# Attention scores from two fp32r pieces in 64-row tiles instead of three bf16 pieces

## The reference

```python
qkv = x @ W_qkv + b_qkv                      # 16 heads, q, k, v of 16 columns each
q, k = rope(q), rope(k)                      # adjacent pairs turned by position
att = softmax(where(causal, q @ k.T / 4, -1e9))
x = layernorm(x + (att @ v) @ W_proj + b_proj)
# 8 experts, the likeliest one for each token, at most 640 tokens each
h = relu(dispatch @ w1[e] + b1[e])           # 256 -> 1024
x = layernorm(x + prob * (h @ w2[e] + b2[e]))
```

## Time and profile before

| | |
|---|---|
| span of the profiled execution | 1587.9 us |
| median of three runs | 1589.46 us |
| PE busy | 1348.4 us (85%) |
| DVE busy | 1197.6 us (75%) |
| ACT busy | 801.6 us (50%) |
| POOL busy | 341.8 us (22%) |
| mean granted TensorE clock | 0.893 |

### The profile page before, as it was taken

One profiled execution on the slowest core, in us unless ns is written; L12 is line 12 of the kernel. 1 busy time (PEld: TensorE's weight loads), 2 busy tenths in 40 slices (PEclk: granted clock), 3 DMA queues, 4 the chain that ended last, 5 costly groups with the idle time before them and its releaser, 6 DMA issues. The chain is left out here.

```text
span 1587.9 us, 26808 instructions
## 1 busy us (share of the span) xinstructions
PE 1348.4 (85%) x7840; PEld 665.9 (42%) x7840; DVE 1197.6 (75%) x2805; ACT 801.6 (50%) x1130; POOL 341.8 (22%) x310
## 2 busy tenths in 40 slices
PE   6766299999998998998999999999577839999987
PEld 3434111233232232332333333321156639999987
DVE  6997499797896887996887978940067638888896
ACT  3443100465665565665665666678534434444442
POOL 3555500001011001001010010110233423344442
PEclk9887555798999999999999999999888759999998
DMA  4586591001202102112002012000245541422220
GB/s 165 175 196 226 147 138 24 2 28 47 63 28 68 43 30 80 37 45 83 27 29 81 28 43 66 8 22 8 72 152 182 172 134 46 128 88 89 85 90 22
DMA packets 117979, 126.95 MB, mean 80 GB/s; under 512 B 14428, under 2 KB 100447, under 8 KB 117856
## 3 DMA queue, kind: packets, MB, share of 16 engines
q1 hardware_dynamic: 114272, 116.97, 25.8%
q0 software_dynamic: 3584, 8.47, 1.5%
HBM read 82.98 MB, written 48.38 MB: 83 GB/s over the span
## 5 line engine op out<-in xcount | busy, mean ns | idle before, releaser
L622 ACT ACTIVATE probs<-scores 128x1024 f32<-128x1024 f32 (+3 forms) x640 | 540.6, 896 | 413.7 <-PE scores L524 413.0
L669 DVE TENSOR_REDUCE part_max<-ring 128x1 f32<-128x512 f32 x768 | 484.4, 685 | 34.2 <-PE ring L552 32.2
L552 PE MATMUL ring<-k_stack,q_stack 96*128 96x512 bf16 (+3 forms) x1280 | 433.8, 384 | 61.9 <-DMA k_stack<-pieces_d 28.4
L524 PE MATMUL scores<-q_stack,k_stack 99*128 99x512 bf16 (+3 forms) x1280 | 344.2, 358 | 13.2 <-ACT probs L622 6.5
L542 PE MATMUL out_p<-probs,v_s 128*32 128x512 f32 (+3 forms) x2560 | 305.7, 550 | 9.3 <-POOL probs L714 5.9
L664 DVE CUSTOM_DVE_ANT_0 scratch<-ring,mask_s 128x384 f32<-128x384 f32 (+3 forms) x512 | 229.3, 488 | 99.3 <-issue 87.1
L552 PEld LDWEIGHTS ring<-k_stack,q_stack 96*128 96x128 bf16 x1280 | 120.7, 99 | 414.4 <-DVE part_max L669 170.1
L714 POOL TENSOR_SCALAR_AFFINE_SELECT probs<-probs 128x512 f32<-128x512 f32 x128 | 81.2, 634 | 863.6 <-ACT probs L622 863.6
L524 PEld LDWEIGHTS scores<-q_stack,k_stack 99*128 99x128 bf16 x1280 | 113.7, 100 | 170.7 <-ACT probs L622 68.1
L1353 PE MATMUL psH<-x_hi,w_hi 128*128 128x384 f32 (+1 forms) x256 | 85.6, 334 | 25.3 <-DVE x_lo L1454 21.9
L195 PE MATMUL psP<-xT,wqk_s 128*128 128x512 f32 x128 | 72.2, 728 | 35.2 <-ACT xT L234 31.4
(11 more groups left out here) (117 smaller groups left out, 1562.9 us busy)
## 6 DMA issues: line engine op xcount, KB each, us to landing
w_whole<-w SPq DMA_DIRECT2D x16, 1024.0 KB, 7.9
q_stack<-pieces_d SPq DMA_DIRECT2D x192, 64.0 KB, 2.7
k_stack<-pieces_d SPq DMA_DIRECT2D x192, 64.0 KB, 2.8
v_d<-vt SPq DMA_DIRECT2D x8, 1024.0 KB, 4.4
v_s<-v_d SPq DMA_DIRECT2D x8, 1024.0 KB, 5.9
o_d<-o_s SPq DMA_DIRECT2D x32, 256.0 KB, 2.1
p_o<-o_d SPq DMA_DIRECT2D x8, 1024.0 KB, 5.8
slots_d<-no_row SPq DMA_DIRECT2D x1, 5200.0 KB, 29.8
```

Source lines behind the costliest of these rows:

```text
L524: last = nc.tensor.matmul(scores[p][:, hh, off:CHUNK], k_stack[i][0:KROWS, j, kb * P:(kb + 1) * P], q_stack[i][0:KROWS, j, c * CHUNK + off ...
L552: nc.tensor.matmul(ring[m % 3][:, 0:w], q_stack[i][0:SROWS, j, qt * P:(qt + 1) * P], k_stack[i][0:SROWS, j, t * CHUNK:t * CHUNK + w], star ...
L622: nc.scalar.activation(probs[n % 2][:, 2 * p:2 * p + 2, off:CHUNK], scores[p][:, :, off:CHUNK], ACT.Exp, scale=SCALE).then_inc(exp_done[p], 1)
L669: nc.vector.tensor_reduce(out, ring[m % 3][:, 0:w], axis=AX.X, op=ALU.max).then_inc(ring_read, 1)
```

## The change

Query and key are cut in two fp32r pieces, and three products (hi-hi, hi-low, low-hi) take the place of six. 48 rows of products and 2 of maxima are 50, so a head fits in 64 rows; heads `2p` and `2p+1` stand in the lower and upper half of the partitions, and the two score matmuls of a pair, or two neighbouring maxima jobs, use different halves of TensorE's rows.

In the projection `mid` and both functions that make it (`rest` on VectorE, `cut_mid` on ScalarE) are gone; `low` is made straight from `raw` and `hi`. Since GpSimd now reads `raw` late, ScalarE waits before it overwrites it. SP stores two pieces of 4 bytes in place of three of 2.

In attention the fold is one reduction; its f32 result is transposed once, and VectorE cuts the transposed rows in two pieces. The rows of ones are written by eight DMAs from a small tile instead of GpSimd's memset. The order of jobs and steps, the plan, the ring and the widths are the same.

```diff
-TERMS = [(0, 0), (0, 1), (1, 0), (1, 1), (0, 2), (2, 0)]
+TERMS = [(0, 0), (0, 1), (1, 0)]
-NPIECE = 3
+NPIECE = 2
+HALF = P // 2
+NPAIR = HPU // 2
 # project_qkv
+            sp.sem_inc(low_ready, 2 * QKG)
-                for n, (ready, piece) in enumerate(((hi_ready, hi), (mid_ready, mid), (low_ready, low))):
+                for n, (ready, piece, start) in enumerate(((hi_ready, hi, 0), (low_ready, low, 2 * QKG))):
             def evacuate(b, c, g):
+                if g == 0:
+                    act.wait_ge(low_ready, QKG * (n + 1))
-                        if g:
-                            cut_mid(b, c, g - 1)
-                    cut_mid(b, c, QKG - 1)
-                if g:
-                    rest(b, c, g - 1)
-                pool.wait_ge(mid_ready, QKG * n + g + 1)
-                nc.gpsimd.tensor_tensor(low[i][:, g, :], rots[i][:, g, :], mid[i][:, g, :],
+                pool.wait_ge(hi_ready, QKG * n + g + 1)
+                nc.gpsimd.tensor_tensor(low[i][:, g, :], raw[i][:, g, :], hi[i][:, g, :],
                                         ALU.subtract).then_inc(low_ready, 1)
 # attention
-        q_stack = [sb(f"q_stack{i}", [P, HPU, T], BF16) for i in range(2)]
+        q_stack = [sb(f"q_stack{i}", [P, NPAIR, T], F32R) for i in range(2)]
-                    rows = slice(r * HS, (r + 1) * HS)
+                    for par in range(2):
+                        rows = slice(par * HALF + r * HS, par * HALF + (r + 1) * HS)
                     for hh in range(2):
-                        j = 2 * p + hh
+                        rows = slice(hh * HALF, hh * HALF + KROWS)
                         last = nc.tensor.matmul(scores[p][:, hh, off:CHUNK],
-                                                k_stack[i][0:KROWS, j, kb * P:(kb + 1) * P],
-                                                q_stack[i][0:KROWS, j, c * CHUNK + off:(c + 1) * CHUNK],
+                                                k_stack[i][rows, p, kb * P:(kb + 1) * P],
+                                                q_stack[i][rows, p, c * CHUNK + off:(c + 1) * CHUNK],
-                nc.tensor.matmul(ring[m % 3][:, 0:w], q_stack[i][0:SROWS, j, qt * P:(qt + 1) * P],
-                                 k_stack[i][0:SROWS, j, t * CHUNK:t * CHUNK + w],
+                rows = slice(j % 2 * HALF, j % 2 * HALF + SROWS)
+                nc.tensor.matmul(ring[m % 3][:, 0:w], q_stack[i][rows, j // 2, qt * P:(qt + 1) * P],
+                                 k_stack[i][rows, j // 2, t * CHUNK:t * CHUNK + w],
             def turn_maxima(u):
-                pe.wait_ge(pieces_ready, u + 1)
-                for s, pieces in enumerate(TURNED):
...
+                pe.wait_ge(fold, u + 1)
+                pe.wait_ge(ring_read, NRING * u + NMAX - 2)
+                nc.tensor.transpose(ring[NMAX % 3][:, 0:P], row_max[:], id_s[:]).then_inc(ring_full, 2)
 # fold_maxima, behind the reduction: four operations and two copies become
+                dve.wait_ge(ring_full, NRING * u + NMAX + 1)
+                turned = ring[NMAX % 3][0:HPU * NQT, 0:P]
+                nc.vector.tensor_scalar(max_rows[0][:], turned, -1.0, None, ALU.mult).then_inc(max_hi_ready, 1)
+                dve.wait_ge(max_hi_ready, u + 1)
+                nc.vector.scalar_tensor_tensor(max_rows[1][:], turned, -1.0, max_rows[0][:],
+                                               ALU.mult, ALU.subtract).then_inc(ring_read, 2)
```

More of the change, by code:

```diff
@@ L87, in project_qkv @@
         xcos = [sb(f"xcos{i}", [P, QKG, CHUNK]) for i in range(2)]
-        hi = [sb(f"hi{i}", [P, QKG, CHUNK], BF16) for i in range(2)]
-        mid = [sb(f"mid{i}", [P, QKG, CHUNK], BF16) for i in range(2)]
-        low = [sb(f"low{i}", [P, QKG, CHUNK], BF16) for i in range(2)]
+        hi = [sb(f"hi{i}", [P, QKG, CHUNK], F32R) for i in range(2)]
+        low = [sb(f"low{i}", [P, QKG, CHUNK], F32R) for i in range(2)]
         vt = [sb(f"vt{i}", [P, TPC, H, VW]) for i in range(2)]
@@ L299, in rope @@
                                         ALU.add).then_inc(roped, 1)
[L301 to L307, removed]
             with dve.Fori(0, B) as b:
@@ L407, in sem @@
             return ctx.enter_context(nc.semaphore(name))
-        q_stack = [sb(f"q_stack{i}", [P, HPU, T], BF16) for i in range(2)]
-        k_stack = [sb(f"k_stack{i}", [P, HPU, T], BF16) for i in range(2)]
+        q_stack = [sb(f"q_stack{i}", [P, NPAIR, T], F32R) for i in range(2)]
+        k_stack = [sb(f"k_stack{i}", [P, NPAIR, T], F32R) for i in range(2)]
         v_s = [sb(f"v_s{i}", [P, NQT, HPU * VW]) for i in range(2)]
@@ L456, in load_chunk @@
                 for r, (qp, kp) in enumerate(TERMS):
-                    rows = slice(r * HS, (r + 1) * HS)
-                    for stack, side, piece in ((q_stack, 0, qp), (k_stack, 1, kp)):
-                        sp.dma_start(stack[i][rows, :, cols],
-                                     pieces_d[b, piece, side, g, :, :, cols]).then_inc(stack_loaded[i][c], 16)
+                    for par in range(2):
+                        rows = slice(par * HALF + r * HS, par * HALF + (r + 1) * HS)
+                        for stack, side, piece in ((q_stack, 0, qp), (k_stack, 1, kp)):
+                            sp.dma_start(stack[i][rows, :, cols].bitcast(F32),
+                                         pieces_d[b, piece, side, g, par, :, :, cols]).then_inc(stack_loaded[i][c], 16)
             def load_v(b, g, i):
@@ L467, in load_max, with load_ones @@
                 for pc in range(NPIECE):
-                    at = (pc % 2) * HPU * NQT
-                    sp.dma_start(q_stack[i][SROWS + pc:SROWS + pc + 1],
-                                 max_rows[at:at + HPU * NQT, pc // 2, :]).then_inc(max_loaded[i], 16)
+                    for par in range(2):
+                        row = par * HALF + SROWS + pc
+                        sp.dma_start(q_stack[i][row:row + 1].bitcast(F32),
+                                     max_rows[pc][par * NPAIR * NQT:(par + 1) * NPAIR * NQT, :].bitcast(F32)
+                                     ).then_inc(max_loaded[i], 16)
+            def load_ones(i):
+                for pc in range(NPIECE):
+                    for par in range(2):
+                        row = par * HALF + SROWS + pc
+                        sp.dma_start(k_stack[i][row:row + 1].bitcast(F32), ones_s[:]).then_inc(ones_loaded, 16)
             def store_o(u, b, g, c):
@@ L496, in _ @@
                 load_v(0, i, i)
+            sp.wait_ge(ones_set, 1)
+            for i in range(2):
+                load_ones(i)
             sp.wait_ge(ring_read, NRING)
@@ L701, in _ @@
         def _(pool):
-            for i in range(2):
-                nc.gpsimd.memset(k_stack[i][SROWS:KROWS], 1.0).then_inc(ones_set, 1)
             with pool.Fori(0, UNITS) as u:
```

74 lines of the change are left out of this document (23 added, 51 removed).

## The result

The changed kernel takes 1641.91 us (median of 4 runs, 1635.18 to 1651.38) against 1588.66 (4 runs of before on the same chip, 1586.74 to 1593.03). The ratio is 1.0337, 95% interval 1.0299 to 1.0374: slower by 3.4%, where I forecast 1480 us. The profiled run took 1635.18 us, its span is 1633.4.

The account below looks back on a forecast made before the run. TensorE was taken to pace full attention steps, with VectorE next. From 1587.9 us, periods -91, last stretch -4, first maxima -1, projection -15 and stores +1 gave 1478, or 1480 us as the runs' median; range 1435 to 1565.

Parts of the forecast that it names:

- Projection: Stage before attention: dropping the subtract and middle piece saves 1.9 us for each of eight chunks, -15 us.
- Overlap of row tiles: Attention scores: a pair's two 64-row tiles run side by side, 0.22 us a pair instead of 0.43.
- rival 2: Attention: row tiles do not overlap, steps stay at 2.88 us, fp32r adds 15 us; 1582 us in all; chance 11%.
- VectorE's floor in full steps: Attention: VectorE becomes the bound, four maxima reads of 0.60 us end to end, 2.40 us a full step.
- rival 3: Attention: half-used rows and gaps lower TensorE's clock; at 40% of time cold, 1645 us in all; chance 9%.
- fp32r's price: Attention matmuls: fp32r runs at the bf16 rate plus some 7 ns each, 2.2 us a unit.
- rival 1: Attention: TensorE's strict order and three-deep ring go on pacing; period 104 us, 1529 us in all; chance 16%.
- Fold: Between units in attention: the reduction chain takes 1.7 us instead of 3.0, with 0.80 for the transpose's round trip.
- Starvation in narrow steps: Attention's 12 narrow steps a unit: VectorE still waits behind TensorE, 6.5 of 18.2 us kept (bounds 0 and 14).
- the 0.15 us for a change of shape: Value product in attention: 1.00 us measured against 0.85 us computed, the difference taken as cost of changing tile shape.
- the last stretch: End of attention, without maxima: ScalarE alone bounds instead of tied with TensorE, -4 us (bounds -10 and +15).
- the first maxima: The 85.8 us of maxima before attention: already VectorE's, only the fold gains there, -1 us.

Follow-up runs that it names:

- bf16_tiles: The changed kernel with bf16 pieces instead of fp32r, all else the same (less precise): 1536.87 us, ratio 0.9672.
- After_fill: The changed kernel with zero rows filling its tiles, 62 rows addressed for maxima and 64 for scores: 1609.42 us, ratio 1.0157.
- bf16_tiles_fill_all_unrolled: The changed kernel in bf16, tiles filled with zero rows, unit loops of VectorE, TensorE and ScalarE written out: 1493.24 us, ratio 0.9416.
- After_fill_all_unrolled: The changed kernel in fp32r, tiles filled with zero rows, unit loops of VectorE, TensorE and ScalarE written out: 1568.01 us, ratio 0.9904.
- after_wide_maxima: The changed kernel with each maxima matmul over all 128 rows and the exponential's scale 0 (maxima wrong): 1787.55 us, ratio 1.1280.

## Why the prediction was wrong

**What was right.** *Projection*: -15 forecast for its end; the first read came 18.1 us earlier, the stage ended near 153.5 (156 forecast). *Overlap of row tiles*: a pair costs 0.24 us; rival 2 is out. *VectorE's floor in full steps*: not in the changed kernel, but in bf16_tiles, with reads of 0.62 us end to end and steps of 2.49 us.

**The step that failed first: the clock, as rival 3 had it.** I gave it 9% because "at 2.4 GHz TensorE would still be at work 2.32 of 2.40 us". That took work for enough. The runs show matmuls over 48 to 67 rows without tiles at 0.50 with TensorE 99% busy, and 80 and 96 rows at 0.93 and 0.96. My own rows held a warning: with maxima alone TensorE was busy 81 of 85.8 us at 0.50. I read that as special to the stage. In the changed kernel the clock reaches 1.00 in full steps (405 to 495), but behind a pause or among short steps it stays at 1.2 GHz for longer than before. The Trainium skill, TensorE: Matmul & The Clock Gate, section The HAM clock gate, has activity release the throttle; 99.13 of 100 us busy at 0.50 disagrees, if busy time is meant, and the measurement decides. The rival's price was a little high: +41 to +70 us for a unit that is always cold gives +12 to +21 at 30%. After_fill gives 118.4 - 113.2 = 5.2 us a period for 0.07 of clock, so the 0.15 up to full speed are worth some 11 us (an estimate, linear from one pair), of which before lost some 3 too. The clock alone would not have made the kernel slower: 118.4 less fp32r's 8.0 us (below) is 110.4 a period against 110.0, with 18 us saved ahead of it (an estimate). That rival 3's 1645 us lies 3 us from the measured 1641.91 is luck: it took 40% at 1.2 GHz where 30% was measured, 55 us for a unit that is always cold where the estimate here gives some 37 (11 / 0.30), and no price for fp32r.

**The second: fp32r's price, and with it rival 1.** I took "the bf16 rate plus some 7 ns" from the earlier trace rows, 2.2 us a unit, hidden. It measured 11.0 us without tiles and 12.2 with (8.0 between the two filled, unrolled kernels, where the clock differs by 0.02 only). My rows were from a stage where one fp32r matmul follows another of the same shape. Here four or five follow a product in 32-column tiles, and the first of them costs 0.34 us instead of 0.23; so does one behind a wait, and the others cost some 20 ns more. The sum also compared 2.32 us of TensorE with 2.40 of VectorE as if each ran alone, and put the wait for the ring at nothing. The step is a circle through both engines, of 2.49 us in bf16 and 2.71 in fp32r, and the margin of 0.08 us was none. So rival 1, which I gave 16%, came true beside rival 3. No run had a deeper ring, so what the circle costs by itself is not shown.

**Two smaller ones.** *Fold*: 3.0 us, not 1.7; the transposition's round trip was priced at 0.80, but TensorE reaches it late (1.95). *Starvation in narrow steps*: 6.5 us assumed; in bf16_tiles_fill_all_unrolled, at clock 0.99 and without the pause, 98.6 - 85.8 - 3.0 = 9.8 us are left beside reads and fold, some of it in full steps of 2.49 instead of 2.40 us.

**A reading that was wrong**: "2 x 512 columns at 2.4 GHz, 0.85 us" for the value product. At the 0.22 us per 512 columns of the earlier trace rows that would be 0.44 us; the trace has the product's second half start 0.45 us behind the first and the next matmul 0.54 us behind that. So the 0.15 us for a change of shape did not follow from it; the price that runs show is the 0.2 us of after_wide_maxima, in fp32r.

**The period put together again**: 97.0 forecast, +1.3 fold, +3.3 starvation, +8.0 fp32r (from the pair at nearly one clock) make 109.6. After_fill_all_unrolled with its 3.0 us pause put back is 106.7 + 3.0 = 109.7 at clock 0.97; that the two agree tests nothing, since the terms were taken from this kernel and its bf16 twin. The clock from 0.97 to 0.85 at 5.2 us for 0.07 is +8.9: 118.5 against 118.4. Only this last step is a test, and its term is a linear estimate from one pair. Seven times 118.4 - 97.0 is 150 us, nearly the whole miss of 162; the rest is the last stretch (+1.2 instead of -4, its clock 0.90 instead of 1.00), the first maxima (+2.1 instead of -1) and 1.4 us behind attention, with 4 us back from the projection; and the median lies 8.5 us above the profiled span, not 1.6.

**What stays open.** The rows are not the clock's whole rule: 96 rows with maxima alone stand at 0.50, which no run here takes apart, and from 48 to 80 rows the shape may change as well. Open are also why steps in the middle of some units fall to 1.2 GHz without a pause (bf16_tiles keeps 0.92 with the pause gone), why the clock is lower in fp32r tiles than in bf16 tiles (0.85 against 0.92), and whether it is the weight load that makes an fp32r maximum slower when none runs ahead of it.

## What to carry to other kernels

Cutting the rows of a matmul saves TensorE nothing by itself, and halved its clock here: look at the granted clock of a first trial with the fewer rows before all else. Where rows must be few, try tiles filled up, with zeros if need be, and count what writing the zeros costs. Take the price of a data type from rows with the same neighbours, since at the start of a burst it is another. When two engines pass a shallow ring to and fro, add up the circle (matmul, read, matmul) and not only each engine's own work. A forecast whose margin on the pacing engine is a few per cent of a step (2.32 against 2.40 us) is a forecast of a tie, and its range has to hold both outcomes.

## What the runs showed of the hardware

- Granted clock in the loop against rows addressed (maxima/scores), bf16, no tiles, same order of matmuls: 96/99 rows 0.96, 80/83 rows 0.93, 64/67 rows 0.51, 48/51 rows 0.50 (TensorE 99% busy between 700 and 800 us in the last two). Rows of zeros count as rows of data (0.96).
- Two 64-row tiles with 48/50 rows each: 0.85 in fp32r, 0.92 in bf16; with 62/64 rows each 0.92 and 0.95.
- An fp32r matmul of 512 columns: some 20 ns over bf16 back to back, and 0.11 us over it as the first after 32-column tiles or behind a wait (recorded 0.50 against 0.39 us); 0.22 us a full step, with and without tiles.
- A change between 64-row tiles and the full array, in fp32r: about 0.2 us each. From a score pair over 67 rows to a maximum over 64, in bf16 at 1.2 GHz: 0.11 us more than from 51 to 48 rows.
- VectorE's loop over units: 3 us from the last instruction of one turn to the first of the next, gone when written out. That was worth 4.2 us a period in before, 3.3 in the bf16 tiles, and 6.1 in after, where the clock fell behind it.
